# A vision tower's layer on one core: the prologue's order, and where the second patch row's token passes stand

## The reference, cut to what matters

```python
patches = X.reshape(B, C, 8, 28, 8, 28).transpose(0, 2, 4, 1, 3, 5).reshape(B, 64, 2352)
tokens = jnp.einsum('bpi,hi->bph', patches, W) + b
h = jnp.concatenate([cls, tokens], axis=1) * pos_embed[None, :, :]
h = h + attn(layernorm(h))      # over the 128 images, for each of 65 positions
h = h + ffn(layernorm(h))       # 8 experts, each takes its 1024 best tokens
```

## Time and profile before

| | |
|---|---|
| median of 3 runs | 1003.63 us (1002.75 to 1004.59) |
| the profiled execution | 1003.19 us |
| its span | 1001.4 us |
| TensorE busy | 736.4 us, 74% |
| VectorE busy | 555.0 us, 55% |
| ScalarE busy | 446.7 us, 45% |
| GpSimd busy | 473.0 us, 47% |
| first token pass | 57.66 us |

### The profile page before, as it was taken

The page is one execution under the profiler, slowest core; times in us unless marked ns, Lnnn a source line. Parts: engine busy times, 40 slices in busy tenths (PEclk is TensorE's granted clock), DMA queues, the critical chain, the costliest instruction groups (busy, mean ns, idle before and its releaser), DMA issues.

```text
span 1001.4 us, 9698 instructions
## 1 busy us (share of the span) xinstructions
PE 736.4 (74%) x2872; PEld 393.2 (39%) x2872; DVE 555.0 (55%) x1238; ACT 446.7 (45%) x729; POOL 473.0 (47%) x486
## 2 busy tenths in 40 slices
PE   0268589999999999999999986533215599997740
PEld 0123235544544454445445543322215355543310
DVE  0210157778778877787787766773787435311110
ACT  0634356656665666576667433221350233232200
POOL 1233444555455555555455222261100648888775
PEclk9779789999999999999999997866555699998875
DMA  9699998898889888988986120000010223443332
GB/s 218 150 206 208 201 205 197 197 217 196 206 197 217 201 202 195 217 192 203 209 195 161 37 64 21 0 22 10 11 11 4 48 58 62 83 65 64 35 34 24
DMA packets 135647, 126.31 MB, mean 126 GB/s; under 512 B 17588, under 2 KB 125996, under 8 KB 135468
## 3 DMA queue, kind: packets, MB, share of 16 engines
q1 hardware_dynamic: 113600, 91.27, 39.6%
q0 software_dynamic: 19456, 33.44, 17.7%
q10 hardware_dynamic: 2540, 0.99, 0.5%
HBM read 87.92 MB, written 12.98 MB: 101 GB/s over the span
## 4 chain that ended last, share of the span: by engine, by line
PE 26%; DVE 24%; POOL 20%; issue 14%; DMA 8%; ACT 5%; SPq 2%; ACTq 1%; POOLq 0%; DVEq 0%
PE bank L1338 10%; POOL out L617 9%; DMA XS<-in_x 5%; POOL XS L606 5%; DVE Y L955 4%; PE bank L1436 3%; DVE stats L905 3%; DVE O L897 2%; DVE XR L897 2%; DVE QT L1030 2%; ACT XS L812 2%; POOL rsB L489 2%; SPq L418 2%; PE bank L1421 2%; PE bank L1467 2%
## 5 line engine op out<-in xcount | busy, mean ns | idle before, releaser
L1338 PE MATMUL bank<-XS,WT 126*128 126x512 f32 (+1 forms) x608 | 313.6, 651 | 34.8 <-DMA XS<-XS 34.8
L794 ACT ACTIVATE XS<-XS 84x1152 f32<-84x1152 f32 (+1 forms) x192 | 187.9, 1028 | 37.0 <-DMA XS<-in_x 35.7
L1338 PEld LDWEIGHTS bank<-XS,WT 126*128 126x128 f32 (+1 forms) x608 | 112.8, 194 | 170.7 <-issue 170.0
L563 POOL COPY XS<-XS 84x1152 f32<-84x1152 f32 x64 | 89.4, 1397 | 84.1 <-DMA XS<-in_x 80.9
L617 POOL DMA_INDIRECT out<-XS x64 | 100.3, 1567 | 24.6 <-issue 18.6
L606 POOL DMA_INDIRECT XS<-token_rows,XS x64 | 65.0, 1016 | 77.2 <-issue 65.4
L576 POOL DMA_DIRECT2D XS<-XS x128 | 70.6, 554 | 55.5 <-PE bank L1338 40.6
L955 DVE TENSOR_TENSOR_SCAN Y<-qdec,XT 128x512 f32<-128x512 f32 (+1 forms) x68 | 77.4, 1158 | 7.8 <-ACT XT L681 7.8
L837 ACT ACTIVATE XS<-bank,VT 128x512 f32<-128x512 f32 x64 | 44.0, 687 | 66.0 <-PE bank L1544 66.0
L1544 PE MATMUL bank<-XS 128*128 128x512 f32 x128 | 66.4, 667 | 0.8 <-ACT XS L681 0.8
L961 DVE SCALAR_TENSOR_TENSOR ET<-Y,ema_c,ET 128x512 f32<-128x512 f32 (+1 forms) x68 | 61.7, 908 | 1.8
(11 more groups left out here) (229 smaller groups left out, 1282.7 us busy)
## 6 DMA issues: line engine op xcount, KB each, us to landing
XS<-in_x SPq DMA_DIRECT2D x192, 392.0 KB
XS<-XS POOLq DMA_DIRECT2D x128, 189.0 KB, 7.7
out<-O SPq DMA_DIRECT2D x16, 256.0 KB, 6.9
token_rows<-XR SPq DMA_DIRECT2D x16, 256.0 KB, 8.1
XS<-in_L_ffn_W SPq DMA_DIRECT2D x16, 256.0 KB, 3.2
XS<-in_L_tok_W SPq DMA_DIRECT2D x1, 1176.0 KB, 10.3
XS<-token_rows,XS POOLq DMA_INDIRECT x64
out<-XS POOLq DMA_INDIRECT x64, 3.3
```

What stands on the lines that cost most here:

```text
L563: pool.tensor_copy(ST[0:ROWS, n % 2, :, :, :].rearrange("p m j r -> p m r j"), px[:, :, :, PASSES:PATCH])\
L794: ins = act.activation(area(slice(0, ROWS), k // 4, piece, m0, m0 + CCOL // 2).rearrange("p m j r -> p m r j"), px[:, :, :, REST * piece:m ...
L1338: ins = pe.matmul(TOK[half][:, :], WT[rows, t, :], area(rows, half, t // REST)[:, :, t % REST, :], start=(t == 0), stop=(t == PASSES - 1))
```

## The change

Three edits in the prologue, one in the passes.

- ScalarE copies chunk 0 ahead of all evacuations, chunk 1 behind those of the projections, chunks 2 and 3 behind the rest. The exp for the scan constants, which waits for the last small loads, goes behind the patch weights' evacuations, and relb, which is evacuated alone, behind it. ScalarE's stage functions are defined in another place, with the same text.
- VectorE rearranges the patch weights without waiting for `c_loaded`, and waits for it behind them. Its wait for VT is on the first evacuation instead of the fifth.
- TensorE's matmul for relb, which needs `c_loaded`, goes behind the patch weights' transposes, with a count of `pe_pro` of its own.
- In iteration 1 the passes are placed by a new table, `FILL_LATE`. Its sum is 19, as that of `FILL`.

```diff
@@ GpSimd, stage w
                 if k == 4 and hy == 0:
-                    pool.wait_ge(*pe_pro.done(7))
+                    pool.wait_ge(*pe_pro.done(8))
@@ ScalarE, prologue
-            act.wait_ge(*c_loaded.done(0))
-            act.activation(ema_t[:, 0:2, :], ema_in[:, 0:2, :], ACT.Exp, scale=-1.0).then_inc(pro_sig.sem, 1)
...
-            for (dst, src), w in zip(evacs, waits):
-                act.wait_ge(*pe_pro.done(w))
-                act.activation(dst, src, ACT.Copy).then_inc(pro_evac.sem, 1)
...
-            for k in range(4):
+            def first_copy(k):
                 for piece in range(C):
                     stage_C(k, piece, 0)
+            def evacuate(n, dst, src):
+                act.wait_ge(*pe_pro.done(n))
+                act.activation(dst, src, ACT.Copy).then_inc(pro_evac.sem, 1)
...
+            first_copy(0)
+            evacuate(0, VT[:, :], bank[5][:, 0:120])
+            evacuate(0, WvT[:, :], bank[5][:, 128:384])
+            evacuate(1, WmT[:, 0:4, :].rearrange("p k d -> p (k d)"), bank[6][:, :])
+            evacuate(2, WmT[:, 4, :], bank[7][:, 0:128])
+            evacuate(2, WhT[:, :, :].rearrange("p k d -> p (k d)"), bank[7][:, 128:384])
+            first_copy(1)
+            for n in range(4):
+                evacuate(3 + n, wt[0:KROWS, 512 * n:512 * n + 512], bank[n][0:KROWS, :])
+            evacuate(7, wt[0:KROWS, 2048:2304], bank[4][0:KROWS, 0:256])
+            evacuate(7, wt[0:ROWS, 2304:2432], bank[4][0:ROWS, 256:384])
+            act.wait_ge(*c_loaded.done(0))
+            act.activation(ema_t[:, 0:2, :], ema_in[:, 0:2, :], ACT.Exp, scale=-1.0).then_inc(pro_sig.sem, 1)
+            evacuate(8, relb[:, :], bank[7][:, 384:512])
+            first_copy(2)
+            first_copy(3)
+            act.wait_ge(*consts_done.done(0))
@@ VectorE
-            dve.wait_ge(*c_loaded.done(0))
             dve.wait_ge(*w_loaded.done(0))
...
+            dve.wait_ge(*c_loaded.done(0))
             dve.wait_ge(*pro_sig.done(0))
...
-            dve.wait_ge(*pro_evac.done(4))
+            dve.wait_ge(*pro_evac.done(0))
@@ TensorE, prologue
-            pe.wait_ge(*c_loaded.done(0))
-            last = pe.matmul(bank[7][:, 384:512], flip, relN, start=True, stop=True)
...
+            pe.wait_ge(*c_loaded.done(0))
+            pe.wait_ge(*pro_evac.done(4))
+            pe.matmul(bank[7][:, 384:512], flip, relN, start=True, stop=True).then_inc(pe_pro.sem, 1)
@@ TensorE, passes
             FILL = {"T": 4, "P": 1, "V": 3, "L": 5, "D": 1, "I": 4, "Q": 1}
+            FILL_LATE = {"V": 4, "L": 6, "D": 2, "I": 4, "Q": 3}
...
-                n = PASSES if s == "end" else (FILL_CLS if a is CLS else FILL).get(s, 0)
+                n = PASSES if s == "end" else (FILL_CLS if a is CLS else FILL_LATE if i == 1 else FILL).get(s, 0)
```

More of the change, by code:

```diff
@@ L655, in _, with stage_C @@
             act.dma_start(lnb[:, :], bass.AP(ln_b.tensor, 0, [[0, 128], [1, D]])).then_inc(c_loaded.sem, 16)
+            def stage_C(k, piece, hy):
+                if piece == C:
+                    return
+                n = CHUNKS * hy + k
+                if piece == 0:
+                    act.wait_ge(*load[n % RING].done(n // RING))
+                    if k % 4 == 0 and begun(hy - 1):
+                        act.wait_ge(*pe_tok[k // 4].done(hy - 1))
+                px = RAW[0:ROWS, n % RING, :].rearrange("p (m r q) -> p m r q", r=2, q=PATCH)
+                m0 = CCOL // 2 * (k % 4)
+                ins = act.activation(
+                    area(slice(0, ROWS), k // 4, piece, m0, m0 + CCOL // 2).rearrange("p m j r -> p m r j"),
+                    px[:, :, :, REST * piece:min(REST * piece + REST, PASSES)], ACT.Copy)
+                if piece == C - 1:
+                    ins.then_inc(copied.sem, 1)
@@ new lines, in first_copy @@
+            def first_copy(k):
+                for piece in range(C):
+                    stage_C(k, piece, 0)
+            def evacuate(n, dst, src):
+                act.wait_ge(*pe_pro.done(n))
+                act.activation(dst, src, ACT.Copy).then_inc(pro_evac.sem, 1)
+            wt = WT[:, :, :].rearrange("p t k -> p (t k)")
+            first_copy(0)
+            evacuate(0, VT[:, :], bank[5][:, 0:120])
+            evacuate(0, WvT[:, :], bank[5][:, 128:384])
+            evacuate(1, WmT[:, 0:4, :].rearrange("p k d -> p (k d)"), bank[6][:, :])
@@ L658, in _ @@
+            evacuate(2, WmT[:, 4, :], bank[7][:, 0:128])
[5 more added lines that the diff above has]
+            evacuate(7, wt[0:ROWS, 2304:2432], bank[4][0:ROWS, 256:384])
             act.wait_ge(*c_loaded.done(0))
             act.activation(ema_t[:, 0:2, :], ema_in[:, 0:2, :], ACT.Exp, scale=-1.0).then_inc(pro_sig.sem, 1)
-            wt = WT[:, :, :].rearrange("p t k -> p (t k)")
@@ L781, in stage_R @@
                 copy(LG[:, gr.position:gr.position + n, :], lg, act_R)
[L783 to L798, removed]
-            for k in range(4):
-                for piece in range(C):
-                    stage_C(k, piece, 0)
             run(act, {"C": stage_C, "T": stage_T, "X": stage_X, "E": stage_E, "F": stage_F, "D": stage_D, "I": stage_I,
@@ L1312, in _ @@
             for k in range(VC):
-                pe.transpose(bank[7][:, 128 + 128 * k:256 + 128 * k], WhN[:, 128 * k:128 * k + 128], ident[:, :])
-            pe.wait_ge(*c_loaded.done(0))
-            last = pe.matmul(bank[7][:, 384:512], flip, relN, start=True, stop=True)
+                last = pe.transpose(bank[7][:, 128 + 128 * k:256 + 128 * k], WhN[:, 128 * k:128 * k + 128], ident[:, :])
             last.then_inc(pe_pro.sem, 1)
```

## The result

| | before | changed |
|---|---|---|
| median of 20 runs | 1002.57 us | 1004.85 us |
| ratio, 95% interval | | 1.0020 (1.0011 to 1.0029) |
| profiled execution's span | 1001.4 us | 1003.1 us |

The changed kernel is slower by 0.2%, and its 1004.85 us lie 0.35 above the forecast's range. One run of 1086.69 us is in the 20; the ratio leaves it out.

The account below looks back on a forecast made before the run. The image-chunk stream bounds 40.4 to 118.4 us, TensorE from 153.7, with a transfer gap before both. Prologue -8.1, first slot +2.5, second +3.1, clock +0.5 give -2.0 us: forecast 1001.6 us, range 996.5 to 1004.5.

Parts of the forecast that it names:

- part 1: Prologue: copying early chunks sooner closes the empty stretch of transfers from 30.0 to 40.4 us, -8.1 us (-8.1 to -6.4).
- the first slot: Second patch row, 118.4 to 153.7 us: three passes more behind stage D, +2.5 us (0 to +3.3); clock -1.0.
- my low end: Prologue gain of only -6.4 us, if ScalarE comes late to a chunk by one evacuation group, 1.7 us.
- The early sign: In the profile after, the first pass at 49.5 us; not there before 51 would make the prologue term wrong.
- The allowance of 0.4: First slot: chunk 15, asked for some 5 us sooner, saves 0.4 us of the 2.9 for later passes.
- Second slot: From 153.7 us: 4.4 us of new holes against 1.36 of old, +3.1 us (+2 to +3.4); clock +1.5.
- No recovery later: Slots behind the second have no more air to take its loss back; slots of 33.9 us as before.
- B: Rival, chance 0.15: TensorE's clock falls in both slots of the second patch row, sum +0.3 us, 1003.9 us.
- C: Rival, chance 0.26: late passes cost little, chunk 15 comes early and the clock stays up, -7 us, 996.5 us.
- D: Rival, chance 0.09: in the prologue, ScalarE's wait for the constants becomes the limit; slower, 1005.7 us and up.
- E: Rival, chance 0.03: the prologue does nothing, as something other than the ring held chunk 3; +6.1 us, 1009.7 us.
- A: The forecast's own case, chance 0.47: prologue and passes nearly cancel, -4 to +1 us, 999.5 to 1004.6 us.

Follow-up runs that it names:

- e9: The kernel before, unchanged, profiled a second time: span 999.4 us, first mark (VectorE's softmax maximum, taken once per slot) at 104.73 us.
- e1: The changed kernel with the old table of passes in every slot, so the new prologue only: 995.68 us against 1001.21 before, ratio 0.9937.
- e10: The kernel before, unchanged, profiled a third time: first mark (VectorE's softmax maximum) at 105.02 us.
- e7: New prologue with the old table, but VectorE waits for the last constant again before making the patch weights: 994.96 us against 1002.78 before.
- e11: Changed kernel, late table only in the second row's second slot, with four useless passes filling its hole: 1012.88 us against 1015.73 before, ratio 0.9979.
- e4: The changed kernel with the late table only in the second slot of the second patch row: 1000.77 us against 1001.21 before, ratio 0.9994.
- e6: New prologue, old table except three more passes ahead of stage D in the second row's first slot: 992.11 us against 1002.78 before, ratio 0.9896.
- e2: The kernel before with the late table in the second row's two slots, old prologue: 1009.22 us against 1001.21 before, ratio 1.0077.
- e5: Changed kernel, old table in the first slot, two late passes moved back early in the second: 998.06 us against 1002.78 before, ratio 0.9953.

## Why the prediction was wrong

The mechanisms were the right ones in the main; the sum of their sizes was 4 us too good. I forecast -2.0 us and got +2.0 (ratio 1.0020). Against a usual execution of before (e9), the changed kernel's marks are 6.0 us early, then 2.8 early, then 2.1 late. Two terms failed: part 1, by about 2 us, and the first slot with its clock, by nearly as much.

1. **Part 1, -8.1: measured -6.3 (e1, 4.8 to 7.7), at the first mark -6.0.** This is the step that failed most; its size was wrong, not its mechanism. I took the empty stretch from one execution and let all of it be gain. In that execution the constants landed late, which widened just the stretch that the change closes: 8.3 us in it, 7.4 and 8.0 in e9 and e10. Of that the changed kernel leaves 0.6 empty, which I had put at nothing. This makes 6.8 to 7.4; the first mark moved by 6.0 and 6.3 against e9 and e10, and where the rest, about 1 us, goes no run shows. The result lies at my low end (-6.4), which I had given to another cause. That cause, ScalarE late to a chunk, did no harm: it had waited 0.36 us when chunk 2 came, at 28.57. The size is known to 1 or 2 us only, as e7's 7.8 us show. The early sign that I had named, the first pass, came even sooner than forecast (47.55, not 49.5) and said nothing of the size: against the first profile chunk 3 came 10.2 us sooner and chunk 4 only 8.0.

2. **First slot, +2.5 with -1.0 for the clock: measured +3.3 (49.2 to 52.5).** D was held by chunk 15, and the three passes behind it cost 2.9 by my count; against e1, D came 0.3 us and the S after it 3.4 us later. The allowance of 0.4 for an earlier chunk 15 was wrong: it came at 131.08, 7.3 us earlier than in the first profile, while the stream was 7.9 ahead before that. The -1.0 for the clock had no row behind it, and the clock fell as before (D's first two matmuls took 2.08 us in both). The wait before D didn't stay "about as long" either, it grew from 3.54 (4.73 in e9, 2.75 in e10) to 6.16 us, since ten passes and not thirteen stand ahead of it. I had the count of passes and didn't carry it into the wait.

3. **Second slot, +3.1 with +1.5 for the clock: measured +4.9.** Right, with the split a little off: 2.7 for the holes (e11) and 2.1 to 2.9 for the clock. The hole of 3.7 us is there (3.69).

4. **No recovery later:** right. The distances behind are those of before.

Of the rivals, B (the clock falls in both slots, +0.3) was what happened, and with part 1 at its measured size B's sum is -6.3 + 2.5 + 3.1 + 2.8 = +2.1. That it comes so close is partly luck: part 1 is not known so well, and the first slot's +2.5 is low while +2.8 for the second slot's clock is at the upper end of what was measured. C fell: chunk 15 on the chain was no sign that it could come sooner; asked for sooner, it took 15.13 us instead of 11.19. D and E fell with e1. The range ended just short of A's upper end, at 1004.5. Part 1's low end together with B's clock, -6.4 + 2.5 + 3.1 + 2.8 = +2.0, would have been 1005.6, and no rival held the two together.

That the new hole lowers the clock agrees with the rule of the Trainium skill named in the prediction (page "TensorE: Matmul & The Clock Gate", section "HAM oscillation — how this bites in real kernels"). In this case the rows of e11 and e4 show that a wait before D of 3.10 us left the clock up once, where one of 2.77 did not.

What stays open: why the last small constants land 1.5 us apart from one execution to the next, in which executions the first slot's clock stays up, and whether passes put ahead of D keep it up. None of these was tried by repeated profiles.

## What to carry to other kernels

Where one wait on an engine's queue holds back a ring of loads, put the copy that frees the ring ahead of it; moving the copies of two chunks was enough here, and VectorE, which was reordered beside it, gave nothing. Filler work belongs into the waits that remain when everything before it has moved: ask which wait is set by a transfer (D's for chunk 15) and fill that one, as e6 did (2.5 us by its rows, the clock left out); work taken out of a place that was covering another engine's latency opens a hole there, and costs its length and the clock besides. And before a gap in one profile is priced, look at the same gap in a second execution.

## What the runs showed of the hardware

TensorE's clock fell in the second slot of every kernel that had the late table there and nothing in its place (changed, e2 and e4 with a hole of 3.69 us, e5 with holes of only 1.77 and 0.74). With the hole filled (e11) the slot has a granted clock of 1.00, as with the old table. Ahead of D it stayed up in e11 through a wait of 3.10 us, with the same table and the same work as in e1, e4 and e10, where it fell around waits of 3.44, 2.77 and 2.75. So the length of a single wait did not tell in these runs whether the clock would fall.

The start of a kernel repeats less well than its slots: the last small load of the same kernel landed at 27.31, 25.79 and 26.39 us, and the distance from the second to the third mark was 33.87 or 33.88 in all three profiles.
